# A fused eight-sequence kernel: in each attention step the turning of probabilities goes in front of the scores or V products

## The reference, cut to what matters

```python
x = L0_attn_X                                   # (8, 512, 256)
xn = _layernorm(x)
Q = (X @ Wq).reshape(n, s, 4, 4, 64)            # 16 heads of width 64, in 4 groups
K = (X @ Wk).reshape(n, s, 4, 64);  V = (X @ Wv).reshape(n, s, 4, 64)
raw = einsum('bsgwe,btge->bstgw', Q, K * scale)
attn = softmax(raw, axis=2)
A = einsum('bstgw,btge->bsgwe', attn, V).reshape(n, s, 1024)
s = X + A @ Wpost
g = silu(mixture_of_experts(xn))                # 64 experts, 8 per row
x = x + s * g
s = state_space_layer(layernorm(x))             # conv, selective scan of 16 states x 512 channels
g = silu(tree_layer(layernorm(x)))              # 8 trees of depth 7
x = x + s * g
```

## Time and profile before

| | |
|---|---|
| median of 3 executions | 2907.19 us (2904.0 to 2913.46) |
| the profiled execution | 2913.83 us, span 2912.0 us |
| TensorE busy (matmul) | 2432.6 us, 84% |
| VectorE busy | 1960.4 us, 67% |
| ScalarE busy | 1831.6 us, 63% |
| GpSimd busy | 1738.0 us, 60% |
| mean granted TensorE clock | 0.929 |

### The profile page before, as it was taken

The page is one execution under the profiler, slowest core; times in us unless marked ns, Lnnn a source line. Parts: engine busy times, 40 slices in busy tenths (PEclk is TensorE's granted clock), DMA queues, the critical chain, the costliest instruction groups (busy, mean ns, idle before and its releaser), DMA issues.

```text
span 2912.0 us, 37618 instructions
## 1 busy us (share of the span) xinstructions
PE 2432.6 (84%) x12740; PEld 1370.6 (47%) x12744; DVE 1960.4 (67%) x2957; ACT 1831.6 (63%) x3334; POOL 1738.0 (60%) x1416
## 2 busy tenths in 40 slices
PE   5777769999788989898989898989898989887771
PEld 3443547775434454444544454445444544453231
DVE  4778835543356776676667676766776777789887
ACT  3456824446477777677667866776777677766752
POOL 1000054426757786777677778766876797655555
PEclk9888879999899999999999998989999999999885
DMA  4000068874555566555654375437543754376767
GB/s 147 23 19 5 16 167 245 238 205 78 81 127 116 105 141 137 109 103 108 154 108 95 80 175 108 88 77 163 118 89 77 169 117 89 79 161 147 176 151 151
DMA packets 282176, 344.96 MB, mean 118 GB/s; under 512 B 66176, under 2 KB 211534, under 8 KB 281984
## 3 DMA queue, kind: packets, MB, share of 16 engines
q0 software_dynamic: 84224, 176.19, 32.8%
q1 hardware_dynamic: 175248, 144.80, 17.2%
q10 hardware_dynamic: 22512, 21.57, 2.2%
HBM read 198.23 MB, written 26.80 MB: 77 GB/s over the span
## 4 chain that ended last, share of the span: by engine, by line
PE 41%; issue 16%; ACT 14%; DVE 14%; POOL 13%; DMA 1%; SPq 1%; another core or an unknown queue 0%; ACTq 0%; POOLq 0%; DVEq 0%
PE bank L1775 6%; PE bank L1764 6%; POOL arena L1651 5%; PE bank L1726 4%; PE bank L1940 4%; PE bank L1911 4%; POOL acc_sb L1629 4%; DVE bank L1539 3%; PE bank L1885 3%; PE bank L1833 3%; ACT PT L1023 2%; PE bank L1787 2%; ACT Pr L1003 2%; POOL arena L1667 2%; POOL arena L1657 2%
## 5 line engine op out<-in xcount | busy, mean ns | idle before, releaser
L1651 POOL TENSOR_TENSOR arena<-arena 128x512 f32<-128x512 f32 x512 | 859.2, 1755 | 16.3 <-DVE arena L1530 10.8
L1629 POOL DMA_INDIRECT acc_sb<-ybuf,slot_idx x256 | 427.1, 1668 | 138.1 <-DMA ybuf<-arena 63.7
L1234 DVE TENSOR_REDUCE negmax<-bank 128x1 f32<-128x512 f32 x512 | 341.4, 682 | 246.4 <-PE bank L1764 245.5
L1657 POOL TENSOR_TENSOR arena<-arena 128x512 f32<-128x512 f32 x192 | 276.0, 1438 | 372.4 <-DVE arena L1539 372.2
L1142 ACT ACTIVATE bank<-arena,A_sb 128x512 f32<-128x512 f32 x512 | 354.7, 696 | 195.3 <-DVE arena L1544 154.7
L1764 PE MATMUL bank<-Kp,Qp 64*128 64x512 f32 x1024 | 413.4, 682 | 64.4 <-ACT Pr L1003 50.9
L1775 PE MATMUL bank<-ident,Pr 128*128 128x128 f32 x2048 | 348.6, 295 | 122.6 <-ACT PT L1023 68.4
L1003 ACT ACTIVATE Pr<-bank,negmax 128x512 f32<-128x512 f32 x512 | 352.9, 689 | 155.7 <-DVE negmax L1234 120.6
L1539 DVE TENSOR_TENSOR_SCAN bank<-bank,arena 128x512 f32<-128x512 f32 x320 | 390.5, 1220 | 73.2 <-ACT bank L1142 68.6
L1023 ACT COPY PT<-bank 128x512 f32<-128x512 f32 x512 | 300.3, 587 | 191.3 <-PE bank L1775 178.9
L1775 PEld LDWEIGHTS bank<-ident,Pr 128*128 128x128 f32 x2048 | 225.6, 146 | 302.7 <-issue 102.3
(11 more groups left out here) (215 smaller groups left out, 3818.4 us busy)
## 6 DMA issues: line engine op xcount, KB each, us to landing
arena<-arena POOLq DMA_DIRECT2D x256, 512.0 KB, 5.4
arena<-bc_dram SPq DMA_DIRECT2D x256, 256.0 KB, 3.9
ybuf<-arena ACTq DMA_DIRECT2D x64, 256.0 KB
arena<-in_w_gate SPq DMA_DIRECT2D x64, 128.0 KB
arena<-in_w_up SPq DMA_DIRECT2D x64, 128.0 KB
arena<-in_w_down SPq DMA_DIRECT2D x64, 128.0 KB
arena<-in_X SPq DMA_DIRECT2D x8, 512.0 KB, 7.1
s_sb<-in_X SPq DMA_DIRECT2D x8, 512.0 KB, 7.5
```

What stands on the lines that cost most here:

```text
L1234: dve.tensor_reduce(negmax[:, m % RING_STAT:m % RING_STAT + 1], bank[m % RING_S_ATT][:, :], AX.X, ALU.max, negate=True).then_inc(att_max, 1)
L1629: pool.indirect_dma_start(acc_sb[:, i, :], None, ybuf, bass.IndirectOffsetOnAxis(ap=slot_idx[:, b * TILES + i, k:k + 1], axis=0), bounds_c ...
L1651: pool.tensor_tensor(st_sb[:, g % RING_S, :], u_sb[:, size_slot(b, cb), :], B_sb[:, load % RING_BC, :], ALU.mult).then_inc(ssm_input, 1)
L1657: pool.tensor_tensor(v, v, C_sb[:, load % RING_BC, :], ALU.mult).then_inc(ssm_c_pool, 1)
```

## The change

On TensorE, `turn_p` of a step is issued first in the step, ahead of the scores (even step) or of the V products (odd step). On ScalarE, the copy of the turned tile goes ahead of the copies of the inverse sums, of Q and of K; the exponential and the widening of the inverse sums stay ahead of it. The counts that the waits compare with move by one where the order asks for it: the bank PROJ may be taken only after the copy of the tile that is now turned before it, and the turning of step at 2, 4 or 6 no longer waits for the other use of that same step, while that of the next step does. No instruction is added, removed or resized, and no DMA is touched.

```diff
@@ ScalarE, att_step
+                m = n - LAG_T
+                if 0 <= m < ATT_STEPS:
+                    place = b * ATT_STEPS + m
+                    w.wait_ge(att_turned, place + 1)
+                    w.wait_ge(att_av, (place - RING_P) // 2 + 1 if m >= RING_P else b * ATT_STEPS // 2)
+                    act.copy(PT[:, m % RING_P, :, :].rearrange("p a b -> p (a b)"), bank[PROBT][:, :]).then_inc(att_pt, 1)
                 if at == 2 and p >= 1:
                     w.wait_ge(att_invmm, PAIRS * b + p)
                     w.wait_ge(att_at, PAIRS * b + p - 1)
@@ -1015,12 +1021,6 @@
                     self.copy_q(b, p + 1, PROJ)
                 if at == 6 and p + 1 < PAIRS and p % 2:
                     self.copy_k(b, (p + 1) // 2, PROJ)
-                m = n - LAG_T
...
@@ TensorE, product_k, product_q, turn_p, spread
-                w.wait_ge(att_pt, b * ATT_STEPS + PAIR_STEPS * (2 * g - 1) + 6 - LAG_T)
+                w.wait_ge(att_pt, b * ATT_STEPS + PAIR_STEPS * (2 * g - 1) + 7 - LAG_T)
-                w.wait_ge(att_pt, b * ATT_STEPS + PAIR_STEPS * (p - 1) + 4 - LAG_T)
+                w.wait_ge(att_pt, b * ATT_STEPS + PAIR_STEPS * (p - 1) + 5 - LAG_T)
-                w.wait_ge(att_q, PAIRS * b + min(p + 1 + (at >= 4), PAIRS))
-                w.wait_ge(att_k, GROUPS * b + min(p + (at >= 6), PAIRS - 1) // 2 + 1)
-                w.wait_ge(att_invbc, PAIRS * b + (p - (at < 2) if p else 0))
+                w.wait_ge(att_q, PAIRS * b + min(p + 1 + (at > 4), PAIRS))
+                w.wait_ge(att_k, GROUPS * b + min(p + (at > 6), PAIRS - 1) // 2 + 1)
+                w.wait_ge(att_invbc, PAIRS * b + (p - (at <= 2) if p else 0))
-                w.wait_ge(att_pt, b * ATT_STEPS + PAIR_STEPS * (p + 1) + 2 - LAG_T)
+                w.wait_ge(att_pt, b * ATT_STEPS + min(PAIR_STEPS * (p + 1) + 3 - LAG_T, ATT_STEPS))
@@ TensorE, att_step
                 p, at = n // PAIR_STEPS, n % PAIR_STEPS
+                if 0 <= n - LAG_T < ATT_STEPS:
+                    self.turn_p(b, n - LAG_T)
                 if n % 2 == 0:
                     if n < ATT_STEPS:
                         self.score(b, n)
@@ -1808,8 +1811,6 @@
                 elif 0 <= n - 1 - LAG_AV < ATT_STEPS:
                     self.values(b, n - 1 - LAG_AV, (2, 3) if self.has_other(p, at - 1) else (0, 1, 2, 3))
-                if 0 <= n - LAG_T < ATT_STEPS:
-                    self.turn_p(b, n - LAG_T)
```

## The result

The changed kernel takes 2973.59 us (median of 4 executions, 2972.84 to 2974.51), the kernel before 2908.44 us (4 executions, 2904.0 to 2913.46): a ratio of 1.0219, 95% interval 1.0207 to 1.0232, or 65 us. The profiled executions have spans of 2971.0 and 2912.0 us; the traces therefore explain 59 us, with the mean granted clock at 0.928 (0.929 before).

The account below looks back on a forecast made before the run. No engine alone bounds the kernel; the streams pull one another, TensorE leading in attention. Bare pairs 28, spreading 3, Q or K products 0 make +31 us, 2938 us against the 2907 us median; range 2880 to 2982 us.

Parts of the forecast that it names:

- The chain in a bare pair: Pairs without spreading, Q or K product: turning, score, maximum, exponential, copy close at 3.83 us against 3.26 us of TensorE work.
- the listed signs: Trace signs: no 3.26 us pairs, VectorE's score wait over 158 us, ScalarE's turning wait falling, no split score pairs.
- the term of the bare pairs: Attention pairs without spreading, Q, K or state product: 70 pairs lose 0.40 us each, 28 us.
- spreading pairs: 56 attention pairs with spreading: TensorE path about 4.1 us, loss 0 to 17 us, taken as 3 us.
- pairs with a Q or K product: 80 attention pairs where the product hides the score chain: 0 us, bounds -40 to +40.
- the time lost behind the decay: Q or K pairs: decay and exponential stand before ScalarE's copy, 2.06 us to the turning's release instead of 1.40.
- the idle time won at Q: Q or K pairs: ScalarE goes straight on from the copy of Q, winning 0.75 us of idle time.
- the 99 us of gaps: TensorE's gaps in six attention stretches (1088 - 989 us), claimed as all that a better order could win there.
- The split scores: 92 score pairs split by an exponential's wait, 1.73 against 1.13 us: joined afterwards, but the wait only moves, net 0.
- The gain: Rival: ScalarE no longer sits behind turnings, a quarter of TensorE's 99 us of gaps goes, 2882 us; chance 0.22.
- The larger loss by scans: Rival: scans and products ahead of the maximum, 1.91 us, enter the chain, about 54 us more, 2992 us; chance 0.13.
- The mechanism held likeliest: Attention: scores lose lead, so a closed chain per pair slows the kernel to 2938 us; chance 0.45 for +9 to +60.

Follow-up runs that it names:

- open version: Changed kernel with turning one step later (LAG_T 3) and ScalarE's copy of the turned tile ahead of the exponential: 2887.02 us, 0.9888 of the kernel before.
- closed version: The changed kernel itself, turning issued first on TensorE, without further edits: 2973.59 us, 1.0219 of the kernel before.
- seq12_after: The change made in the first two of the eight sequences only, against the kernel before: ratio 1.0074.
- lag3_after: Changed kernel with the turning one step later against the scores (LAG_T 3 in place of 2): 1.0255 of the kernel before.

## Why the prediction was right and wrong

**Right: sign and mechanism.** The chain in a bare pair is 3.84 us, predicted 3.83. Of the 41 bare pairs without state products in the same stretch 13 stood at 3.25 to 3.28 us before; after the change none is below 3.84 us, the lowest quarter stands there, and the median is 4.36. Each of the listed signs came: no pair of 3.26 us, VectorE's wait for scores 268 us, ScalarE's wait for turnings 48 us, its exponential's wait for the maximum 106 us (49.7 us before, in the same list of waits), no split score pairs, the wait at the turning.

**Wrong: the size, in the term of the bare pairs.** The forecast was +31 us, measured +65 (59 in the traces). The term of the bare pairs, 70 x 0.40 = 28 us, measured 52 us (37.7 + 14.5). Three things in it failed. First, the chain at 0 was costed without the widening, which is on ScalarE between the exponential and the copy: 4.36 us, not 3.83. I had named it as standing ahead of the copy and left it out of the sum. The floor at 6 was right, and in sequences 3 to 8 those pairs cost nothing on average (103.2 to 102.2 us); at 0 they cost 27.0 us (196.1 to 223.1). The 21 of them without a state product went from 3.88 to 4.90 us on average, 1.02 us each where 0.40 had been taken. Second, I scaled the count from the sequences behind 800 us to all eight, and the first is another case: its bare pairs alone lost 23 us (75.7 to 98.8), 9.38 us each at 0 where the mean had been 7.51. It runs beside the experts' routing, and there the maximum has long work of VectorE ahead of it. One such pair at 0, first in the kernel before, then after:

```profile
192.67 1.44 PE L1764 MATMUL bank<-Kp,Qp 64*128 64x512 f32 x4
198.13 1.12 PE L1764 MATMUL bank<-Kp,Qp 64*128 64x512 f32 x2
203.20 0.69 DVE L1234 TENSOR_REDUCE negmax<-bank 128x1 f32<-128x512 f32 x1
...
209.21 1.13 PE L1764 MATMUL bank<-Kp,Qp 64*128 64x512 f32 x4
218.29 0.68 DVE L1234 TENSOR_REDUCE negmax<-bank 128x1 f32<-128x512 f32 x1
221.94 2.08 PE L1764 MATMUL bank<-Kp,Qp 64*128 64x512 f32 x4
```

Before, the next scores start 5.46 us after these although their maximum starts only after 10.53; after, they start behind the maximum, 12.73 us later. After the change the maxima of the seven pairs at 0 of this sequence start 27 us late in total (against 1.16 us behind the scores), and the next scores wait for all of it; the spreading pairs behind them got 9.9 us shorter in return. Third, shortening a link gives back only part of its price (about 8 us for 0.40 us of widening), so pairs are not each held by one chain, and floor times count does not give the size. This last is argued from the runs, not isolated.

**Wrong, but nearly cancelling (+7 us together):** pairs with a Q or K product, set to 0 between -40 and +40, measured +24.0 and -4.6. That the time lost behind the decay outweighed the idle time won at Q is what the traces suggest, not isolated: in sequences 3 to 8, pairs without a state product, the two turnings behind the copy of Q stood 1.42 us apart (medians) before; after, they stand 1.82 us apart where one decay starts within the pair, 2.44 us where two do; ScalarE's wait for Q products rose from 74.5 to 98.3 us. The spreading pairs, set to +3, won 22.2 us, nearly half of it in sequence 1 (70.0 to 60.1), where the pairs at 0 just before them lost 13.1. Their path was costed at about 4.1 us; the shortest takes 4.37 us before and 4.81 after. The first two pairs of each sequence, not costed, lost 12.6 us, and no run isolates why. Each of these terms was off by 5 to 25 us, and that they nearly cancelled is luck.

**The sentence on the 99 us of gaps was wrong.** It took TensorE's gaps in the earlier trace rows as all that an order could win. The busy time of 989 us held waiting: a split score pair is shown busy for 1.73 us for the work of 1.13. The open version shows 336 us of score time against 413, and its attention of sequences 3 to 8 is 30 us shorter than before (1036.0 against 1066.0). The Trainium skill says in Perfetto Trace Analysis, Identifying the Most-Contended Engine, that matmul busy time is a bad measure of how near a kernel is to the peak, because pipelined matmuls look smaller in the trace. The trace agrees that it misleads, but by this other way: half of the array's rows idle and the record says busy.

**The split scores.** "The same wait moved, net 0" was right in its direction for the closed version: TensorE lost the 100 us of score time and got none of it back as time. With the ring open part of it is a gain. The Trainium skill's rule in TensorEngine Tiling (Array Packing), Key Properties, that tiles of the array work independently, was right in both kernels (a joined pair takes 1.13 us, a split one 1.73); whether it pays was decided by the ring.

**The rivals.** The gain did not come: ScalarE did stop waiting for turnings (139 to 48 us), but waited for maxima and Q products instead. The larger loss by scans came near in size (2992 us) and not in cause: seq12_after loses a third without any scan of the state steps, and in the pairs at 0 of sequences 3 to 8 VectorE makes up 8 of the 40 us above the ring. But in sequence 1 other work of VectorE ahead of the maximum did go into the chain, which is this rival's mechanism in a place where it was not looked for. The mechanism held likeliest, under-sized, is what happened.

## What to carry to other kernels

When an order of in-order engines is changed, follow the newest item round: from its first engine over all hand-overs, and over what stands ahead of it in each engine's stream, back to the place where the next item waits. If that ring closes within one period, its sum of latencies is a floor for the period, whatever the busy shares say; every instruction in between counts, and each tie must be cut for it to open (here the lag of the turning and the place of a copy: the one alone gave 1.0255, the other 1.0182, both 0.9888, where the changed kernel is at 1.0219). Check the depth of every buffer ring when a lag is changed, for it can close a new one.

## What the hardware showed that was not expected

- Busy time of TensorE can hide waiting: 1024 score matmuls of 64 rows fill 413.4, 313.3 or 336.4 us (before, after, open version) at 0.68 to 0.69 us each, by whether the two halves of the array are used at once: 1.13 us for a joined pair, 1.73 us for a split one.
- The hand-overs are as long as the work: from the start of a score pair to its maximum 1.16 us, from maximum to exponential 0.72 to 0.73, exponential to a copy behind it in the same stream 0.67, copy to the turning it releases 0.69, in the two rings shown (after, lag3_after) within 0.05 us. A copy that stands in front of an exponential instead delays it by only 0.48 us (1280.60 to 1281.08), less than its own 0.59.
- The second, short instruction that reads an exponential's row sum (0.20 us) lies within the 0.67 us to the copy, and the turning starts 0.84 us after the exponential's start (1281.08 to 1281.92) when nothing else holds it.
